# New engine orders for an adaLN block with attention and a mixture of experts, and 23 instead of 15 filler products

## The reference

```python
mod = (_silu(L0_c) @ L0_wmod).reshape(L0_c.shape[0], 6, 1, -1)
sa, ca, ga, sb, cb, gb = (mod[:, 0], mod[:, 1], mod[:, 2], mod[:, 3], mod[:, 4], mod[:, 5])
ga = (2 * (ga >= 0) - 1) * jnp.maximum(jnp.abs(ga), 0.25)   # gb in the same way
h = _layernorm(x, axis=-1) * (1 + ca) + sa
x = x + ga * attention(h)
h = _layernorm(x, axis=-1) * (1 + cb) + sb
x = x + gb * experts(h)
```

## Time and profile before

| | us |
| --- | --- |
| median of 3 runs | 372.43 (372.35 to 372.51) |
| the profiled execution | 372.05 |
| its span, first to last instruction | 370.2 |
| PE busy | 348.0 (94%) |
| ACT busy | 306.6 (83%) |
| DVE busy | 295.6 (80%) |
| POOL busy | 227.4 (61%) |
| mean granted TensorE clock | 0.989 of 2.4 GHz |

### The profile page before, as it was taken

How to read it: one execution, slowest core, us unless ns; L and a number is a source line. 1 busy time by engine, 2 the same in 40 slices (tenths; PEclk the granted TensorE clock), 3 DMA queues, 4 the chain that set the end, 5 groups by cost and what they waited for, 6 DMA issues and landing times.

```text
span 370.2 us, 9794 instructions
## 1 busy us (share of the span) xinstructions
PE 348.0 (94%) x3300; PEld 306.4 (83%) x3300; DVE 295.6 (80%) x1063; ACT 306.6 (83%) x524; POOL 227.4 (61%) x220
## 2 busy tenths in 40 slices
PE   2977989999999999999999999999999999998996
PEld 2756868888889889888888889888888989986985
DVE  2798698989797977879798789889898978747643
ACT  3567699999898989999999899899986969885840
POOL 3246758397738858584747839385668756274651
PEclk9998799999999999999999999999999999999999
DMA  5055017270624435053805224170706042325482
GB/s 172 31 152 227 2 56 318 51 237 11 198 83 144 143 117 172 6 181 105 266 23 189 98 112 179 40 247 4 255 5 224 8 140 92 123 110 152 166 267 74
DMA packets 19112, 47.94 MB, mean 129 GB/s; under 512 B 2603, under 2 KB 6390, under 8 KB 18806
## 3 DMA queue, kind: packets, MB, share of 16 engines
q1 hardware_dynamic: 18432, 46.64, 37.8%
q10 hardware_dynamic: 630, 0.67, 0.6%
HBM read 42.82 MB, written 4.48 MB: 128 GB/s over the span
## 4 chain that ended last, share of the span: by engine, by line
PE 53%; DVE 25%; issue 12%; POOL 3%; ACT 3%; DMA 1%; ACTq 1%; DVEq 0%; POOLq 0%
PE pY L1054 17%; PE pH L1038 5%; PE pH L1040 5%; PE pH L1039 5%; PE pQV L1001 3%; DVE x_all L1461 3%; DVE v L1519 3%; DVE st L1467 2%; DVE qn L1432 2%; DVE qsum L1423 2%; PE pQV L978 2%; PE pQV L962 2%; PE pC L1008 2%; PE pQV L964 2%; PE pQV L963 2%
## 5 line engine op out<-in xcount | busy, mean ns | idle before, releaser
L1054 PE MATMUL pY<-wout,v 128*128 128x128 f32 x1024 | 132.7, 278 | 0.4 <-DVE v L1519 0.2
L1054 PEld LDWEIGHTS pY<-wout,v 128*128 128x128 f32 x1024 | 124.5, 191 | 6.6 <-DVE v L1519 1.9
L746 ACT ACTIVATE u<-pH,cols 128x512 f32<-128x512 f32 x128 | 85.4, 686 | 17.4 <-PE pH L1040 12.8
L427 POOL TENSOR_TENSOR v<-u,gate_bc 128x512 f32<-128x512 f32 x48 | 67.4, 1410 | 17.5 <-PE pY L1054 10.7
L1519 DVE TENSOR_TENSOR v<-u,gate_bc 128x512 f32<-128x512 f32 x80 | 64.3, 812 | 9.0 <-DMA gate_bc<-route_scratch 5.7
L1038 PE MATMUL pH<-h_hi,win_hi 128*128 128x512 f32 x128 | 58.9, 460 | 1.5 <-ACT u L746 1.5
L1040 PE MATMUL pH<-h_lo,win_hi 128*128 128x512 f32 x128 | 50.4, 394 | 0.0
L1039 PE MATMUL pH<-h_hi,win_lo 128*128 128x512 f32 x128 | 50.4, 394 | 0.0
L439 POOL TENSOR_TENSOR h_lo<-h,h_hi 128x512 fp32r<-128x512 f32 x16 | 20.7, 1293 | 35.5 <-ACT h_hi L674 35.5
L746 ACT ACT_TABLE_LOAD x27 | 34.6, 1283 | 0.5
L444 POOL TENSOR_TENSOR rstd<-ve,neg_half 128x4 f32<-128x4 f32 x16 | 19.3, 1203 | 24.8 <-DVE nm L1476 24.8
(11 more groups left out here) (156 smaller groups left out, 780.6 us busy)
## 6 DMA issues: line engine op xcount, KB each, us to landing
gate_bc<-route_scratch SPq DMA_DIRECT2D x64, 512.0 KB, 5.0
x_all<-in_L_attn_x SPq DMA_DIRECT2D x16, 256.0 KB, 5.0
out<-x_all SPq DMA_DIRECT2D x15, 256.0 KB, 2.1
gates<-gate_scratch SPq DMA_DIRECT2D x1, 1792.0 KB, 6.6
route_scratch<-gateT SPq DMA_DIRECT2D x64, 4.0 KB
gb_bc<-gb_scratch SPq DMA_DIRECT2D x1, 1024.0 KB, 8.0
win<-in_L_ffn_w_in SPq DMA_DIRECT2D x1, 512.0 KB, 5.2
wout<-in_L_ffn_w_out SPq DMA_DIRECT2D x1, 512.0 KB, 6.4
```

What stands on the lines that cost most here:

```text
L427: pool.tensor_tensor(v[:, e % U, :], u[:, e % U, :], gate_bc[:, b % 2, e, :], ALU.mult).then_inc(s["vp_done"], 1)
L746: act.activation(u[:, e % U, :], pH[:, e % 2, :], ACT.Gelu_apprx_tanh, bias=cols[:, e:e + 1]).then_inc(s["gelu_done"], 1)
L1054: i = mm(pY[:, t * P:(t + 1) * P], v[:, e % U, t * P:(t + 1) * P], wout[:, e, :], start=False, stop=(e == NE - 1), skip_group_check=True)
```

## The change

Every engine's list is replaced: beginnings, step functions and ends. No step's instructions change, and each is issued as often as before, but for `keep_clock`: 23 calls instead of 15. The loops cover other batches. The router and state products were in column groups (16 small products over four 32-wide groups) before already. The diff, cut to the step functions and the beginnings:

```diff
@@ -294,66 +294,69 @@
 
             def step(b):
                 load_x(b + 5)
-                if b == -1:
-                    spread_later_gates()
-                if has(b):
-                    spread_gates(b, 3)
                 store_gates(b + 1)
                 spread_gates(b + 1, 0)
                 spread_gates(b + 1, 1)
+                spread_gates(b + 1, 2)
+                spread_gates(b + 1, 3)
                 if has(b):
                     store_out(b)
-                if b == -1:
-                    spread_moe_gates()
-                spread_gates(b + 1, 2)
 
             load_x(1)
             load_x(2)
+            load_experts()
+            load_x(3)
             store_mod_gates()
-            load_x(3)
             spread_first_gates()
-            load_experts()
+            store_moe_gates()
             load_expert_bias()
-            store_moe_gates()
-            for b in range(-1, 9):
+            spread_moe_gates()
+            spread_later_gates()
+            for b in range(-1, 8):
                 step(b)
+            load_x(13)
+            store_gates(9)
...
@@ -446,199 +449,182 @@
                 pool.tensor_tensor(nmr2[:, :], nm2[:, :], rstd2[:, :], ALU.mult).then_inc(s["nmr2_ready"], 1)
 
             def step(b):
-                if has(b + 3):
-                    gated_weight(b + 3)
-                if has(b):
-                    weigh(b, 1)
+                if has(b + 1):
+                    weigh(b + 1, 1)
+                if has(b + 5):
+                    rstd_L(b + 5)
                 if has(b + 2):
-                    rstd_O(b + 2)
-                if has(b):
-                    weigh(b, 3)
-                if has(b + 1):
-                    h2_low(b + 1)
-                if has(b):
-                    weigh(b, 5)
-                if has(b + 4):
-                    h_low(b + 4)
-                if has(b + 2):
-                    rstd_B(b + 2)
-                if has(b + 3):
-                    gated_const(b + 3)
+                    h2_low(b + 2)
                 if has(b):
                     residual2(b)
+                if has(b + 4):
+                    gated_weight(b + 4)
+                if has(b + 3):
+                    rstd_O(b + 3)
+                if has(b + 1):
+                    weigh(b + 1, 3)
+                if has(b + 4):
+                    gated_const(b + 4)
+                if has(b + 1):
+                    weigh(b + 1, 5)
+                if has(b + 3):
+                    rstd_B(b + 3)
                 if has(b + 5):
-                    rstd_L(b + 5)
-
+                    h_low(b + 5)
+
...
+            rstd_L(0)
+            rstd_L(1)
+            h_low(0)
             masks()
-            rstd_L(0)
-            h_low(0)
-            rstd_L(1)
+            expert_low()
+            rstd_L(2)
             gated_weight(0)
             h_low(1)
+            gated_const(0)
+            rstd_O(0)
+            gated_const(1)
             gated_weight(1)
-            gated_const(0)
-            rstd_L(2)
-            rstd_O(0)
+            rstd_B(0)
             rstd_L(3)
             h_low(2)
-            rstd_B(0)
-            expert_low()
-            gated_const(1)
+            h2_low(0)
             gated_const(2)
-            h2_low(0)
             rstd_O(1)
-            gated_const(3)
-            rstd_L(4)
             gated_weight(2)
...
 
             def step(b):
+                ln2_apply(b + 1)
+                gelu(b, 1)
+                gelu(b, 2)
+                sw_evac(b + 2)
+                qT_evac(b + 2)
                 h2_evac(b + 1)
+                gelu(b, 3)
+                gelu(b, 4)
+                out_square(b + 2)
+                exp_router(b + 1)
                 ln1_apply(b + 4)
-                gelu(b, 4)
+                exp_k(b + 3)
                 gelu(b, 5)
-                exp_k(b + 3)
-                exp_router(b + 1)
+                ek_evac(b + 3)
                 gelu(b, 6)
-                ek_evac(b + 3)
+                gateT_evac(b + 1)
+                exp_q(b + 3)
                 gelu(b, 7)
-                exp_q(b + 3)
+                gelu(b + 1, 0)
                 h_evac(b + 4)
-                gateT_evac(b + 1)
-                gelu(b + 1, 0)
-                gelu(b + 1, 1)
-                sw_evac(b + 3)
-                qT_evac(b + 3)
-                ln2_apply(b + 2)
-                gelu(b + 1, 2)
-                out_square(b + 3)
-                gelu(b + 1, 3)
 
...
@@ -1055,232 +1061,263 @@
                 i.then_inc(s["mm2_done"], 1)
 
             def step(b):
-                combine(b, 1)
-                ek_back(b + 3)
                 hidden(b, 7)
-                combine(b, 2)
+                hT(b + 4)
+                hidden(b + 1, 0)
                 combine(b, 3)
-                hidden(b + 1, 0)
-                if has(b + 4):
-                    hT(b + 4)
-                gate_turn(b + 1)
                 combine(b, 4)
-                hidden(b + 1, 1)
-                state(b + 3)
                 combine(b, 5)
                 combine(b, 6)
+                state(b + 3)
+                hidden(b + 1, 1)
+                hidden(b + 1, 2)
                 state_weights(b + 3)
                 q_turn(b + 3)
                 combine(b, 7)
-                if has(b + 4):
-                    kT(b + 4)
-                hidden(b + 1, 2)
+                kT(b + 4)
+                h2T(b + 2)
+                hidden(b + 1, 3)
+                hidden(b + 1, 4)
                 attend_centred(b + 3)
-                hidden(b + 1, 3)
-                h2T(b + 2)
-                hidden(b + 1, 4)
+                logits(b + 2)
                 moe_bias(b + 1)
+                attend_project(b + 3)
                 hidden(b + 1, 5)
-                if has(b + 4):
-                    qv(b + 4)
-                attend_project(b + 3)
-                logits(b + 2)
+                hidden(b + 1, 6)
+                qv(b + 4)
                 combine(b + 1, 0)
-                hidden(b + 1, 6)
+                ek_back(b + 4)
+                combine(b + 1, 1)
+                combine(b + 1, 2)
+                gate_turn(b + 2)
 
             turn_weights()
...
             turn_weights()
             modulation()
             hT(0)
+            keep_clock()
             gain_centred()
+            keep_clock()
             residual_gates()
             keep_clock()
-            keep_clock()
-            keep_clock()
             kT(0)
+            keep_clock()
             qv(0)
             keep_clock()
             keep_clock()
             keep_clock()
+            keep_clock()
+            keep_clock()
             ek_back(0)
             keep_clock()
             keep_clock()
             hT(1)
-            keep_clock()
             state(0)
             q_turn(0)
             state_weights(0)
+            keep_clock()
+            attend_centred(0)
             kT(1)
-            attend_centred(0)
+            keep_clock()
+            attend_project(0)
             keep_clock()
             qv(1)
-            keep_clock()
             ek_back(1)
-            attend_project(0)
+            keep_clock()
             keep_clock()
             hT(2)
+            keep_clock()
+            keep_clock()
+            keep_clock()
+            keep_clock()
+            keep_clock()
             state(1)
-            keep_clock()
-            keep_clock()
+            h2T(0)
+            keep_clock()
+            kT(2)
+            state_weights(1)
+            logits(0)
             q_turn(1)
-            state_weights(1)
-            kT(2)
+            keep_clock()
+            hidden(0, 0)
             attend_centred(1)
-            keep_clock()
-            h2T(0)
+            hidden(0, 1)
             qv(2)
-            logits(0)
             ek_back(2)
-            attend_project(1)
-            hidden(0, 0)
-            hT(3)
-            hidden(0, 1)
-            state(2)
             hidden(0, 2)
             gate_turn(0)
-            state_weights(2)
...
@@ -1540,247 +1577,277 @@
                                   gb_bc[:, b, :].unsqueeze(1).to_broadcast([P, T, P]), ALU.mult).then_inc(s["yg_ready"], 1)
 
             def step(b):
-                if has(b + 2):
-                    ln2_stats(b + 2)
-                if has(b + 3):
-                    q_inv(b + 3)
-                if has(b + 2):
-                    ln2_var(b + 2)
-                if has(b + 3):
-                    state_out(b + 3)
-                    q_norm(b + 3)
-                gates_turned(b + 1)
-                if has(b + 3):
-                    k_inv(b + 3)
-                weigh(b, 7)
-                y_gated(b)
                 if has(b + 5):
                     ln1_stats(b + 5)
                     ln1_var(b + 5)
+                gates_turned(b + 1)
                 weigh(b + 1, 0)
+                y_gated(b)
                 if has(b + 4):
                     k_max(b + 4)
```

(32 more changed lines are left out.)

757 lines of the change are left out of this document (413 added, 344 removed).

## The result

Before 372.35 us (median of 5 runs, 370.22 to 372.51), after 379.45 (378.75 to 383.68), ratio 1.024, 95% interval 1.019 to 1.029. The forecast was 370.0, and 379.45 lies above its range. The profiled execution took 383.68; the other four agree within 0.8 us at 379, so some 4 us of what its trace shows are its own, and no second trace of this kernel tells which.

What follows compares the result with a forecast made beforehand. PE was taken as the bound, 348.0 of 370.2 us busy, ACT second in the middle. Terms -1.5 - 0.6 - 0.6 + 0.3 = -2.4; 372.05 - 2.4 + 0.38 = 370.0 us, forecast range 368.3 to 371.6, overall 366.8 to 375.0.

Steps and rivals of the forecast that it cites:

- the middle: Rounds after the beginning: same instructions, slightly less wait before q_turn, gain 0.05 us a round over 12 rounds, 0.6 us.
- Both signs: Prediction wrong if the first y_gated comes less than 1 us earlier than 73.55, or rounds are longer than 20.8 us.
- Step 1: Beginning, DVE: q_sum(0) now ahead of expert_gates, so 1.1 us earlier for it, q_norm(0), q_turn(0) and attend_centred(0).
- Steps 2 and 3: Beginning: residual1(0) at about 27.5, 3.5 us earlier; then batch 0's second norm before exp_q(1), hidden(0, 0) at 37 to 39.
- Step 4: Beginning: gates land at 42.4 to 44, POOL stands at gated_const(2); 1.2 us or nothing of the 7 us lead left.
- Step 5: Beginning, PE: h2T(1) at 51.5, 3.6 us earlier with 2.4 us more work open; 1.5 us gain taken.
- rival B: Beginning's lead spent at gated_const(2), middle as before: 372.2 us, no measurable change; chance 0.13.
- Step 6: Beginning, PE: 8 added filler calls fill the thin stretch, no stretch at 1.2 GHz; effect inside the 1.5 us.
- The end: Last products on PE: order changes only which goes first; 0 us, from -1 to +1.
- C: Rival: slower, q_norm waits behind h_low in every round, 12 rounds at 0.4 us more: 375.4 us; chance 0.13.
- D: Rival: slower, ACT the bound in batches 0, 1 and 11 through added table loads: 375.0 us; chance 0.10.

Runs made afterwards that it cites:

- half_gates: The changed kernel, orders untouched, with echosen alone in PSUM and elg_cut left in SBUF: 370.36 us, ratio 0.997 to the kernel before.
- psum_new_start: Orders of the changed kernel until about 75 us, those of the kernel before from there, elg_cut and echosen in PSUM: 373.73 us, ratio 1.001.
- psum_old_start: Orders of the kernel before until about 75 us, those of the changed kernel from there, elg_cut and echosen in PSUM: 366.20 us, ratio 0.986.
- psum_gates: The changed kernel, orders untouched, with elg_cut and echosen in PSUM instead of SBUF: 366.92 us, ratio 0.990; run again 366.61 us, ratio 0.983.
- psum_before: The kernel before, orders untouched, with elg_cut and echosen in PSUM: 371.33 us, ratio 1.000.

## Why the prediction was wrong

**The failed step is the middle**: "the instructions of a round are the same ... every wait but one has slack", with a gain of 0.6 us and -6 and +4 as its bounds. Measured, the eleven rounds took 12 us more (241.4 against 229.2), and 379.45 us lies above every rival's time too. Both signs that the prediction gave for being wrong came: the first y_gated not earlier, the rounds longer than 20.8. The counts of instructions are the same, the durations aren't. I had named the meeting of DVE and POOL for q_norm and h_low alone, one instruction a round, and looked for it only where the order put those two side by side. The step that was moved onto a running POOL queue was gates_out, whose last operations need each other and so can meet POOL once each: +17.2 us of DVE, 1.1 a batch. That the rounds grew by 1.1 us on average as well is chance in part: without the first round they grew by 0.7 each. Three runs bear it out: the same orders without the meeting (12.5 us less than after), the same edit without the orders (no change), and half of it (9 us less). So the meeting cost 12.5 us, more than the 7.1 by which the change was slower: it also hid what the new orders win.

The Trainium skill (SBUF — State Buffer, "Who interferes with whom") has the rule that I cited for q_norm, and the runs agree with it: two SBUF inputs against a GpSimd instruction that reads SBUF, the second one blocks until the first is done. The groups of half_gates agree, 817 ns against 191. It also lists tensor_scalar among the operations that can take the shared ports with one input, and the 2.37 us of L1341 agree.

**Step 1** (q_sum(0) 1.1 us earlier): it came at 23.36, 2.4 us later than in rows 6. I subtracted what had gone from in front of it and didn't add what had come: k_max(0) started at 19.64, and at 15.76 before. Of these 3.9 us 2.2 are L1341 beside win_lo (2.37 us for 0.21); the rest goes with the statistics of batches 1 and 2, which now stand ahead, the first behind a wait of 1.74 us for x. **Steps 2 and 3** rest on it: residual1(0) at 31.4 in place of 27.5, hidden(0, 0) at 41.1 in place of 37 to 39, 4.1 us earlier than before where 6 to 8 were expected.

**Step 4** was right in mechanism:

```profile
45.29 1.29 POOL L406 TENSOR_TENSOR x_all<-x_all,gates 128x512 f32<-128x512 f32 x1 [4.24 <-DMA gates<-gate_scratch]
```

The gates landed at 45.3 where 42.4 to 44 were expected, being issued at 35.3 instead of 33.3; residual1(1) came at 48.4, not 44.8 to 46.4. **Step 5** (net gain 1.5): h2T(1) at 54.8, where 51.5 was expected and 55.11 was before; psum_new_start, and psum_old_start beside psum_gates, put the whole beginning at about 0. That is rival B's half of the story. **Step 6** was right for the kernel after: its clock is 1.00 from 0 to 60 us, where rows 5 had 0.50. In psum_gates, with the same fillers, it is 0.91 from 40 to 60, so they don't hold it up in every case. **The end** was put at 0, from -1 to +1: it is 1.2 us longer in the kernel after (89.95 against 88.77) and 3.1 to 3.4 shorter once the operands are in PSUM.

**The rivals.** C (q_norm late every round) did not happen: the idle time before q_turn fell from 4.2 to 1.3 us, though q_norm itself went from 779 to 836 ns. D (table loads) did not either: in psum_gates, with all 61 loads, PE is busy 40.93 us of 281.4 to 322.6, and it was 41.00 before:

```profile
281.40:322.60 41.20, 40.93 (x414) 37.12 (x415) 31.40 (x108) 37.42 (x62) 27.41 (x25) 1.00 0.41 134
```

The right answer was of C's kind (a meeting of DVE and POOL, in most rounds) at another step, and above C and D in price: a chain of four can meet POOL up to four times, as in batch 9, where the four took 1.13, 1.20, 1.30 and 1.22 us.

**What I did not see on the gain side.** With the lock out of the way the new orders are worth 1.0 to 1.7%, 4 to 6 us, against 2.4 forecast, and hardly by fewer waits: after 60 us PE idles 4.4 us in psum_before and 3.8 in psum_old_start. From one step's start to the next one's, without the idle time, PE's steps after 62 us add up to 294.6 us in psum_before and 290.9 in psum_old_start. In that count combine has 1.1 us of the 3.7. Its group shows more (psum_before 132.6 us for its 1024 products, this one 127.0), because busy times of neighbours overlap:

```profile
L1268 PE MATMUL pY<-wout,v 128*128 128x128 f32 x1024 | 127.0, 276 | 1.0 <-DVE v L1985 1.0
```

The rest is at the joints, with gains and losses. attend_project takes 0.98 us when logits follows and 0.81 when hidden follows, which gives 1.6 us in all; but logits now follows attend_centred, which went from 0.81 to 0.98 and costs 2.0. gate_turn (0.13 to 0.03), q_turn, hidden, hT and state_weights win 0.8 to 1.2 us each, moe_bias loses 1.4. So a step's price on PE depends on its neighbour, which my count of equal instructions left out. This is read from two traces; no run isolates it.

## What to carry to other kernels

When an order changes, look for chains of small dependent VectorE operations with both inputs in SBUF, and ask what GpSimd has in its queue at that moment: here each link could cost one whole GpSimd operation (1.0 to 1.3 us), and the work that is released by the step just ahead of the chain is what it will meet. If the place of the chain is fixed by someone who waits for it, move an operand to PSUM instead of the step. And when a step is said to come earlier, add up all that now stands in front of it, not only what has left.

## What the runs showed of the hardware

- An operation of 0.18 to 0.20 us took up to 1.33 behind a GpSimd operation, in batch 9 four in a row with the last operation of 0.23; with one input in PSUM it took 0.18 to 0.20 at the same place. Writing to PSUM with both inputs in SBUF did not help (817 ns).
- Freeing the first links moved the wait to the last: 287 to 627 ns.
- Two executions of one kernel differed by 2.0 us in one 16x128 operation, as it started 0.20 us behind win_lo or 0.28 ahead of it.
- Two waits of 1.04 and 1.70 us on PE were followed by ten microseconds at a mean granted clock of 0.71: in that execution the stall cost about as much again as it lasted (10 x 0.29 = 2.9 us).
- 12.5 us were won with 14.0 us less busy time on DVE (19.2 less in gates_out), an engine that is 82% busy.
